# The last ten output projections of a recurrence, made inside the attention that follows

## The reference, cut to what matters

```python
o = _rmsnorm(o, g_norm_w) * g * jax.nn.sigmoid(g)     # o: states of the scan over the sequence
x = x + _bitlinear(o, w_o, nw_o)                      # rms norm, rows rounded to 8 bits, product with ternary w_o
xn = _layernorm(x)                                    # (x - mean) / sqrt(var + 1e-5), by rows
q = split_heads(xn @ Wq + bq); k, v = heads of ctx @ Wk + bk, ctx @ Wv + bv     # 16 heads of 16, 154 keys
x = x + softmax(q k^T / 4) v @ Wo + bo
```

## Time and profile before

| | us |
|---|---|
| median of 3 runs | 1428.05 (1425.85 to 1431.0) |
| the profiled execution: its time | 1432.4 |
| its span, first to last instruction | 1430.7 |
| mean granted TensorE clock, of 2.4 GHz | 0.946 |
| recurrence and attention, by the lines' times | about 807 to 1077 |

### The profile page before, as it was taken

How to read it: one execution, slowest core, us unless ns; L and a number is a source line. 1 busy time by engine, 2 the same in 40 slices (tenths; PEclk the granted TensorE clock), 3 DMA queues, 4 the chain that set the end, 5 groups by cost and what they waited for, 6 DMA issues and landing times. The chain is left out here.

```text
span 1430.7 us, 27678 instructions
## 1 busy us (share of the span) xinstructions
PE 1296.7 (91%) x9691; PEld 1037.2 (72%) x9691; DVE 1010.1 (71%) x2014; ACT 882.9 (62%) x2215; POOL 457.0 (32%) x628
## 2 busy tenths in 40 slices
PE   4979999999699999989999866689988699999997
PEld 3534444436599999977888654578877699999995
DVE  4687878734566665556788687578875688888773
ACT  4427666774476666645121467478873688888883
POOL 5311222218444333326000356311100244444430
PEclk8979999999899999999999987599998799999998
DMA  4655422200000000003000210022203577777755
GB/s 91 189 122 138 68 46 47 47 1 5 30 2 2 1 2 1 2 6 121 1 0 1 75 24 1 23 62 47 51 10 107 187 232 232 232 233 233 230 158 188
DMA packets 97916, 116.15 MB, mean 81 GB/s; under 512 B 23549, under 2 KB 83187, under 8 KB 97779
## 3 DMA queue, kind: packets, MB, share of 16 engines
q1 hardware_dynamic: 88323, 99.83, 25.7%
q0 software_dynamic: 4416, 12.06, 2.6%
q10 hardware_dynamic: 5040, 2.49, 0.7%
HBM read 88.47 MB, written 16.55 MB: 73 GB/s over the span
## 5 line engine op out<-in xcount | busy, mean ns | idle before, releaser
L827 ACT ACTIVATE sa_probs<-ps 128x512 f32<-128x512 f32 (+1 forms) x304 | 154.5, 577 | 87.6 <-PE ps L780 86.4
L851 DVE TENSOR_REDUCE sa_top<-ps 128x2 f32<-128x1024 f32 (+3 forms) x160 | 171.8, 1114 | 40.9 <-PE ps L756 25.5
L2738 PE MATMUL ps<-me_h,me_w_parts 128*128 128x256 f32 x1104 | 140.9, 288 | 4.8 <-issue 2.9
L2738 PEld LDWEIGHTS ps<-me_h,me_w_parts 128*128 128x128 f32 x1104 | 137.3, 193 | 6.4 <-issue 3.1
L2752 PE MATMUL ps<-me_w_parts,me_mid 128*128 128x256 f32 x1104 | 136.3, 283 | 0.0
L2752 PEld LDWEIGHTS ps<-me_w_parts,me_mid 128*128 128x128 f32 x1104 | 132.4, 188 | 0.0
L3246 ACT ACTIVATE room<-ps,cx_top 128x154 f32<-128x154 f32 x256 | 96.6, 391 | 35.4 <-DVE cx_top L3295 34.9
L2819 DVE TENSOR_TENSOR me_w_parts<-me_chunk,me_w_parts 128x1024 fp32r<-128x1024 f32 x92 | 110.4, 1222 | 9.9 <-ACT me_w_parts L2779 8.3
L2803 ACT ACTIVATE me_full<-ps,me_b 128x256 f32<-128x256 f32 x184 | 95.2, 518 | 34.7 <-PE ps L2738 34.5
L2849 DVE TENSOR_TENSOR me_mid<-me_full,me_mid 128x256 fp32r<-128x256 f32 x184 | 89.9, 506 | 34.7 <-ACT me_mid L2805 34.6
L3125 POOL TENSOR_TENSOR room<-room 128x512 f32<-128x512 f32 x64 | 67.1, 1049 | 140.7 <-DVE room L3303 140.6
(11 more groups left out here) (466 smaller groups left out, 3370.5 us busy)
## 6 DMA issues: line engine op xcount, KB each, us to landing
me_chunk<-in_L_ffn_W_dram SPq DMA_DIRECT2D x92, 512.0 KB, 4.1
sa_k<-scr_k SPq DMA_DIRECT2D x48, 128.0 KB, 4.5
sa_q<-scr_q SPq DMA_DIRECT2D x96, 64.0 KB, 4.7
cn_qd<-cn_qh SPq DMA_DIRECT2D x60, 64.0 KB, 2.0
scr_q<-room SPq DMA_DIRECT2D x6, 512.0 KB, 5.6
scr_k<-room SPq DMA_DIRECT2D x6, 512.0 KB, 5.8
me_b<-in_L_ffn_b_dram SPq DMA_DIRECT2D x23, 128.0 KB, 3.6
x<-in_x_dram SPq DMA_DIRECT2D x4, 512.0 KB, 6.0
```

Of the source, the lines that this page charges most:

```text
L827: act.activation(probs[:, step % self.PROBS, h0:h0 + many, 0:w], src[:, :, 0:w], ACT.Exp, scale=DH ** -0.5).then_inc(exped.sem, 1)
L851: dve.tensor_reduce(top2[:, k % 2, k0 // 512, h0:h0 + many, sb % HBLK], src[:, :, 0:w], AX.X, ALU.max).then_inc(freed.sem, 1)
L2738: last = pe.matmul(ps[:, MID + n % 4, 0:RT], w[:, u % 2, 0, i, DM * k + P * b:DM * k + P * b + P], h[:, u % 2, j, k, :], start=(m == 0), s ...
```

## The change

The recurrence makes the outputs of tiles 0 to 5 only, and its loop ends at step 18, with three steps more for the preparation of the attention (TAIL). The outputs of tiles 6 to 15 move into the attention's block, each through `Q_BANK`, between two pairs of queries: tiles 6 to 9 behind pair 1, 10 to 13 behind pair 2, 14 and 15 behind pair 3 (WINDOWS). `turn_x` of the next pair waits for the last of them. What they need is kept: `zo`, the scales, a copy of `w_o`. The planner gets items for each piece, and GpSimd rounds their rows at the block's head and behind the gathers of tiles 0 and 1. Inverse deviations of tiles 0 and 1 are made by square root in steps 16 and 17, those of tiles 2 to 5 at the block's head, and those of tiles 6 to 9 and 10 to 15 by four Newton steps on GpSimd, behind the gathers of tiles 2 and 4. VectorE makes the normal rows of tiles 2 to 15. The weight passes move from steps 15 to 17 to steps 2 to 4, and pair 0's pieces from steps 21 to 24 to steps 18 and 19.

```diff
 def recurrent(c, rec, nx):
-    STEPS = NT + LAG
+    STEPS = NT + 3
+    EARLY = STEPS - LAG
...
+                pool.tensor_copy(nx.w_o[:, :, :], wt[:, 3, :, :]).then_inc(s["kept"].sem, 1)
+                pool.tensor_copy(nx.magic[:, :], magic[:, :]).then_inc(s["kept"].sem, 1)
-                for k in range(STEPS):                      # on every engine
+                for k in range(STEPS + nx.TAIL):
...
-                    if k + 3 >= LAG and k + 3 < STEPS:
+                    if 0 <= k + 3 - LAG < EARLY:
...
 class CrossNarrow:
+    TAIL = 3
+    KEPT = NT - 10
+    WINDOWS = {1: range(6, 10), 2: range(10, 14), 3: range(14, 16)}
+    PARTS = ((6, 10), (10, 16))
...
     def pool_step(self, pool, k):
-        if k == 15:                                         # scale wq; wol: 16 -> 3, wql: 17 -> 4
+        if k == 2:
...
-        if k in (19, 20):
+        if k == 17:
             self.wait(pool, "inverted", 1)
-            for t in (2 * k - 38, 2 * k - 37):
+            for t in (0, 1):
...
     def tensor_step(self, pe, k):
-        if k == 21:
+        if k == 18:
             self.turn_x(pe, 0)
-        if k in (22, 23):
-            self.queries(pe, 0, k - 22)
+        if k == 19:
+            self.queries(pe, 0, 0)
+            self.queries(pe, 0, 1)
...
     def turn_x(self, pe, g):
+        if g - 1 in self.WINDOWS:
+            self.wait(pe, "o_add", self.WINDOWS[g - 1][-1] + 1 - self.KEPT)
...
     def scalar_step(self, act, k):
+        if k == 16:
+            self.wait(act, "shifted", 1)
+            act.activation(self.sd[:, 0:2], self.ve[:, 0:2], ACT.Sqrt).then_inc(s["rooted"].sem, 1)
         if k == 18:
-            self.wait(act, "shifted", 1)
-            act.activation(self.sd[:, 0:4], self.ve[:, 0:4], ACT.Sqrt).then_inc(s["rooted"].sem, 1)
-        if k == 21:
             self.high_x(act, 0)
-        if k == 23:
+        if k == 19:
             self.high_q(act, 0)
-        if k == 24:
             self.query_copies(act, 0, 2)
...
+    def o_round(self, pool, o):
+        pool.tensor_scalar(self.zo[:, o, :], self.zo[:, o, :], self.times_o[:, o:o + 1], ROUND, ALU.mult, ALU.add
+                           ).then_inc(self.s["o_round"].sem, 1)
+
+    def o_turn(self, pe, o):
+        n = o - self.KEPT
+        self.wait(pe, "o_round", n + 1)
+        for g, tiles in self.WINDOWS.items():
+            if o == tiles[0]:
+                self.wait(pe, "ql", g + 1)
+        if n:
+            self.wait(pe, "o_add", n)
+        for d in range(KD):
+            last = pe.transpose(self.c.ps[:, self.Q_BANK, P * d:P * d + P], self.zo[:, o, P * d:P * d + P], self.c.ident[:, :])
+        last.then_inc(self.s["o_turn"].sem, 1)
+
+    def o_evict(self, act, o):
+        n = o - self.KEPT
+        self.wait(act, "o_turn", n + 1)
+        act.activation(self.qt[:, :], self.c.ps[:, self.Q_BANK, 0:D], ACT.Identity, bias=self.magic[:, 1:2]
+                       ).then_inc(self.s["o_evict"].sem, 1)
+
+    def o_product(self, pe, o):
+        self.wait(pe, "o_evict", o - self.KEPT + 1)
+        for d in range(KD):
+            last = pe.matmul(self.c.ps[:, self.Q_BANK, D:2 * D], self.qt[:, P * d:P * d + P], self.w_o[:, d, :],
+                             start=(d == 0), stop=(d == KD - 1))
+        last.then_inc(self.s["o_product"].sem, 1)
+
+    def o_add(self, dve, o):
+        n, s, x = o - self.KEPT, self.s, self.c.x[:, o, :]
+        self.wait(dve, "o_product", n + 1)
+        dve.scalar_tensor_tensor(x, self.c.ps[:, self.Q_BANK, D:2 * D], self.unit_o[:, o:o + 1], x, ALU.mult, ALU.add
+                                 ).then_inc(s["o_add"].sem, 1)
+        self.wait(dve, "o_add", n + 1)
...
+        dve.bn_stats(self.o_stats[:, n % 2, :], x).then_inc(s["o_seen"].sem, 1)
+        self.wait(dve, "o_seen", n + 1)
+        dve.bn_aggr(self.c.rowstat.mv[:, o, :], self.o_stats[:, n % 2, :]).then_inc(s["o_mean"].sem, 1)
+
+    def o_rstd(self, pool, i):
...
+        self.wait(pool, "o_half", i + 1)
+        then(pool.tensor_scalar(y.bitcast(I32), self.half[:, a], -1.0, float(0x5f3759df), ALU.mult, ALU.add))
+        for n in range(4):
+            then(pool.tensor_tensor(w, y, y, ALU.mult))
+            then(pool.tensor_tensor(w, w, v, ALU.mult))
+            then(pool.tensor_scalar(w, w, -0.5, 1.5, ALU.mult, ALU.add))
+            if n < 3:
+                then(pool.tensor_tensor(y, y, w, ALU.mult))
+        pool.tensor_tensor(self.rstd[:, a], y, w, ALU.mult).then_inc(s["inverted"].sem, 1)
...
     def order(self):
+            if t in (2, 4):
+                add(("o_rstd", t // 2 - 1, 0), "POOL", 3.5, [("gather", t, 0), ("o_var", t // 2 - 1, 0)])
...
         for g in range(1, NPAIR):
...
+            for o in self.WINDOWS.get(g, ()):
+                add(("o_turn", o, 0), "PE", 0.24, [("o_round", o, 0), ("low_q", g, 0)]
+                    + ([("o_add", o - 1, 0)] if o > self.KEPT else []))
+                add(("o_evict", o, 0), "ACT", 0.38, [("o_turn", o, 0)])
+                add(("o_product", o, 0), "PE", 0.24, [("o_evict", o, 0)])
+                add(("o_add", o, 0), "DVE", 0.85, [("o_product", o, 0)])
...
```

More of the change, by code:

```diff
@@ L141, in average, with done @@
         dve.bn_aggr(self.mv[:, t, :], self.stats[:, t % 2, :]).then_inc(self.averaged.sem, 1)
-    def done(self):
-        self.measured.passed(NT)
-        self.averaged.passed(NT)
+    def done(self, tiles=NT):
+        self.measured.passed(tiles)
+        self.averaged.passed(tiles)
 class LayerNorm:
@@ L1757, in recurrent @@
             "forget_t", "scanned", "back", "sq_h", "u", "sq_u", "zo", "top_o", "o_chain", "square", "sigma", "o_scaled",
[L1758 removed]
+            "round_o", "added", "kept")}
         def at(eng, name, n):
@@ L1872, in _ @@
                 nx.tensor_keys(pe)
-                for k in range(STEPS):
+                for k in range(STEPS + nx.TAIL):
                     if k + 1 < STEPS:
@@ new lines, in o_var, with then @@
+    def o_var(self, dve, i):
+        a, s = slice(*self.PARTS[i]), self.s
+        self.wait(dve, "o_mean", self.PARTS[i][1] - self.KEPT)
+        dve.tensor_scalar(self.ve[:, a], self.c.rowstat.mv[:, a, 1], EPS, None, ALU.add).then_inc(s["o_var"].sem, 1)
+        self.wait(dve, "o_var", i + 1)
+        dve.tensor_scalar(self.half[:, a], self.ve[:, a].bitcast(I32), 1, None, ALU.arith_shift_right).then_inc(s["o_half"].sem, 1)
+    def o_rstd(self, pool, i):
+        a, s, link = slice(*self.PARTS[i]), self.s, self.o_link
+        v, y, w = self.ve[:, a], self.guess[:, a], self.work[:, a]
+        def then(instruction):
+            instruction.then_inc(link.sem, 1)
+            pool.wait_ge(link.sem, link.next())
+        self.wait(pool, "o_half", i + 1)
[7 more added lines that the diff above has]
+        pool.tensor_tensor(self.rstd[:, a], y, w, ALU.mult).then_inc(s["inverted"].sem, 1)
@@ L3686, in order @@
             add(("laid", g, 0), "SP", 7.5, [("low_q", g, 0)] + behind)
+            for o in self.WINDOWS.get(g, ()):
[4 more added lines that the diff above has]
+                add(("o_add", o, 0), "DVE", 0.85, [("o_product", o, 0)])
+                for i, part in enumerate(self.PARTS):
+                    if o == part[1] - 1:
+                        add(("o_var", i, 0), "DVE", 0.3, [("o_add", o, 0)])
         add(("m_bias_turn", 0, 0), "PE", 0.15, [("low_q", NPAIR - 1, 0)])
@@ L3940, in _ @@
                         self.high_x(act, t)
+                    elif what == "o_evict":
+                        self.o_evict(act, t)
                     elif what == "m_w_t":
@@ L4028, in _ @@
                         front.add_gate(dve)
+                    elif what == "o_add":
+                        self.o_add(dve, t)
+                    elif what == "o_var":
+                        self.o_var(dve, t)
                     else:
-                        if t == 4:
+                        if t == 2:
                             dve.wait_ge(rooted.sem, rooted.at(2))
-                            dve.reciprocal(self.rstd[:, 4:NT], self.sd[:, 4:NT]).then_inc(self.s["inverted"].sem, 1)
+                            dve.reciprocal(self.rstd[:, 2:6], self.sd[:, 2:6]).then_inc(self.s["inverted"].sem, 1)
                             dve.wait_ge(self.s["inverted"].sem, self.s["inverted"].at(2))
+                        for i, part in enumerate(self.PARTS):
+                            if t == part[0]:
+                                self.wait(dve, "inverted", i + 3)
                         normal(t)
```

87 lines of the change are left out of this document (59 added, 28 removed).

## The result

The changed kernel takes 1457.53 us (median of 4 runs, 1454.19 to 1465.2), the kernel before 1427.26 (4 runs, 1425.85 to 1431.0): the ratio is 1.0215, with a 95% interval of 1.0167 to 1.0264, 30.3 us slower. The forecast was 9.4 slower. The direction was right, the size a third of what came.

What follows compares the result with a forecast made beforehand. Outputs ending the recurrent stage, then query copies, were taken to bound the attention. 7.7 us won and 17.1 lost gave +9.4: 1441.8 against the profiled 1432.4, which stood 4.35 above the median 1428.05, so 1437.5 us; range 1422 to 1445.

Steps and rivals of the forecast that it cites:

- The front: Join of recurrent stage and attention: pair 0's queries end the stage, first scores at 909.6 for 917.28, 7.7 us won.
- S: Time of the attention's first scores, from which later times are counted; forecast at 909.6.
- Tile 2 at S + 26.0: Attention: tile 2's first scores come 26.0 us behind the attention's first scores, as in the kernel before.
- The window of 11.6 us: Query bank between pairs 1 and 2: four output tiles at 2.9 us each, bounds 7.6 and 16 for the four.
- Turn to high queries, 12.3 us: Pair 2 behind the first window: turned at S + 29.4, high queries end near S + 41.7, copies 9.16 more.
- Newton's 4.8 us a group: GpSimd in the attention: 17 dependent instructions at 0.28 us, 4.8 us for each of two groups, bounds 2.4 to 9.5.
- Weight passes: Recurrent stage, steps 2 to 4: GpSimd's three moved passes, 4.5 us in all, fit in idle time and cost nothing.
- Added work at nothing: Attention: ten output tiles' engine work is covered by holes and costs nothing; 8.2 us if all on TensorE's path.
- Absorbed: Rival, attention windows: four tiles take 9.2 us, pairs go the short way, tile 4 only 2.6 late; 1423 us, chance 0.20.
- even: Rival, attention: only tile 4 late by about 8, or 8.2 us of TensorE on the path; 1428.5 us, chance 0.22.
- GpSimd holds tile 5: Rival, attention: the second Newton group ends at S + 78.5 and delays tile 5's weighing; 4 us more, 1441.5, chance 0.08.
- The clock falls: Rival, TensorE in the attention: lower clock for some 5 us in each of two holes; 5 us more, 1442.5, chance 0.05.

Runs made afterwards that it cites:

- Bank first: Changed kernel with 0.5 us planning precedence for both the windows' output tiles and the query links of pairs 1 to 3: 1431.23 us, 1.0004 of the kernel before.
- the kernel before with precedence: The kernel before, planned without the delays that hold back the query links of pairs 1 to 3: 1427.59 us, 0.9977 of the kernel before.
- the halves: Two runs of the changed kernel with 0.5 us precedence: output tiles alone, 1458.63 us; query links of pairs 1 to 3 alone, 1448.45 us.
- four moved tiles with precedence: Changed kernel with twelve output tiles in the recurrent stage, four in one window, and small precedence for window and pairs 1 and 2: 1425.21 us, 0.996.
- ten (0.9991): Changed kernel with precedence of 0.2 us for output tiles and 0.3 for query links of pairs 1 to 3: 1428.3 us, 0.9991 of the kernel before.
- none moved: All sixteen output tiles in the recurrent stage, early weight passes and pair 0 query chain kept, planner of the kernel before with precedence: 1426.42 us, 0.997.
- filled: Changed kernel with 16, 24 and 32 matmuls that nothing reads ahead of the scores of tiles 2, 4 and 6: 1464.67 us.
- filled less: Changed kernel with 16 matmuls that nothing reads ahead of tile 2's scores, 12 ahead of tile 4's, none ahead of tile 6's: 1456.7 us.

## Why the forecast had the sign and not the size

**The front** was right: S = 909.1 against 909.6, by the steps given (high queries end at 902.51, forecast 902.5; SP's last copies 907.6, forecast 907.6). From A the gain is 9.2, so the fit has luck in it: the chain from A took 1.5 less than forecast (29.2 for 30.7, with A at 878.89), and A itself came 1.0 later in this trace (879.92).

**Tile 2 at S + 26.0** was wrong by 3.2, by the mishap named at the end of the prediction: pair 1's high part lost its place ahead of the Exps.

**The window of 11.6 us** is the step that failed: it took 18.6, above the upper bound of 16. The 1.9 for a bare chain is right (the two tiles of the last window are added at 995.44 and 997.48, 2.0 apart), but 2.9 took a fixed order for a small surcharge of 1.0 a tile; measured, it was 2.7. An add of 0.47 us waits as long as what stands ahead of it in VectorE's order waits, and for tile 7 that was a copy; tile 9 stood behind tile 2's own work on three engines.

**Turn to high queries, 12.3 us,** took 14.6, and the copies 10.0 in place of 9.2 (that 0.8 is the one long issue, chance as far as the traces show). Tile 4 was to be 11.5 late; 3.2 more for tile 2, 7.0 for the window, 2.3 for the links and 0.8 for the copies make 24.8, and the trace has 24.9 (S + 64.3 for S + 39.4). The second window adds more in the same way, 15.6 from low queries to turn (964.48 to 980.05) and 29.9 between tiles 4 and 6 for a forecast 24.9. Tiles 6 and 7 took 15.5, forecast 15.4, and the third window was done before it was needed: both right. So 35.6 were lost where 17.1 stood in the sum.

**Newton's 4.8 us a group** was right: first to last step, from 951.35 to 956.06, 4.7. **Weight passes** can't be told from nothing: A stands at 875.2 to 879.9 in the twelve traces that have them early, at 877.5 and 878.9 in the two that don't. **Added work at nothing** was right as long as the holes were there; without them it is 9.0, near the 8.2 that the prediction gave for TensorE's path, and as near the 8.9 that it gave for VectorE.

**The rivals.** *Absorbed* named both things that decide, a window of 2.3 a tile and the high part ahead of the Exps. Bank first has them nearly (2.6 and at once), and even then the sum is *even*: the work comes onto the path, and 1431.2 and 1428.3 were measured where 1428.5 was given. *GpSimd holds tile 5* did happen (the second group ends at 1003.8, and tile 5's gather follows at 1004.45), but 3.4 us less of each group were worth 1.5 at most. *The clock falls* did happen, 0.50 from 973.4 to 980.0; the runs price the first hole at 0.4 us or less and the second at about 1.5, not 2.5 each.

The Trainium skill ("Perfetto Trace Analysis", Identifying the Most-Contended Engine) was the page behind absorbed: by weight loads there was room, since they are busy 57.38 of 70.1 us in the kernel before with precedence. The added work took 9.0 us all the same. Whether TensorE's matmuls or VectorE's work used that room up no run here shows, so the page is neither borne out nor refuted.

## What to carry to other kernels

Where engines follow an order that is fixed beforehand, price a moved chain by what stands ahead of each of its links there, not by its links and a surcharge; and give precedence to the whole chain, as the half left behind takes back most of what the other saves (-0.9 and 7.4 us for the halves, 25.0 for the whole).

Moving work out of a tail pays only while the tail is what ends the stage: here a tile gave 1.25 us at the front until the query chain ended it (29.1 us behind A), cost 0.8 to 0.9 in the attention, and four moved tiles with precedence (0.996) stand ahead of ten (0.9991). Ahead of none moved they stand by 1.2 us, which these runs can't tell from nothing.

## What the runs showed of the hardware

Behind the hole ahead of tile 4 the granted clock was 0.50 for 6.6 us, although TensorE was busy in 6.30 of them. It had fallen inside the hole, in which TensorE ran nothing:

```profile
970.60:973.40 2.80, 0.01 (x1) 0.02 (x1) 0.00 (x0) 0.00 (x0) 0.00 (x0) 0.50 0.38 94
973.40:980.00 6.60, 6.30 (x24) 4.88 (x25) 5.47 (x13) 4.64 (x15) 0.00 (x0) 0.50 0.00 1
```

That is the lower of the two levels, 1.2 GHz. With 24 matmuls that nothing reads in this hole, the 6.6 us behind it ran at 1.00 (filled). It is no sure way: the same 16 of them ahead of tile 2 went with 1.00 behind them in filled and with 0.85 in filled less. The Trainium skill ("TensorE: Matmul & The Clock Gate", Part 1) says that the throttled level is the default and activity lifts it; these rows agree in kind.

The time to issue a copy of 64 KB on SP's queue was 0.60 us in nearly all cases, and 1.0 to 1.8 in single ones; one of these made 0.8 us of the difference between two traces.
